# Second attention block of a fused transformer kernel: one 96-row product per head over moved keys and queries, values spread over the steps, and splits moved in the first block

## The reference, cut to what matters

```
x = layer_norm(hidden, ln1_w, ln1_b)                      # 8 x 100 x 512
q = (x   @ q_w + q_b).reshape(B, 100, 16, 32)
k = (ctx @ k_w + k_b).reshape(B, 361, 16, 32)
v = (ctx @ v_w + v_b).reshape(B, 361, 16, 32)
attn = softmax(where(mask, q k^T / sqrt(32), min))
hidden = (attn v) @ cproj_w + cproj_b + hidden
out = hidden + gelu(layer_norm(hidden, ln2_w, ln2_b) @ fc_w + fc_b) @ proj_w + proj_b
```

## Time and profile before

| | |
|---|---|
| median of 3 runs | 2333.56 us (2332.52 to 2339.51) |
| the profiled execution's own time | 2332.67 us |
| its span | 2330.9 us |
| mean granted TensorE clock | 0.985 of full speed |
| PE, DVE, ACT, POOL busy | 95%, 69%, 51%, 41% of the span |
| second block's logits, first to last | 1822.2 to 2159.7 us |

### The profile page before, as it was taken

The page is one execution under the profiler, slowest core; times in us unless marked ns, Lnnn a source line. Parts: engine busy times, 40 slices in busy tenths (PEclk is TensorE's granted clock), DMA queues, the critical chain, the costliest instruction groups (busy, mean ns, idle before and its releaser), DMA issues.

```text
span 2330.9 us, 37139 instructions
## 1 busy us (share of the span) xinstructions
PE 2206.4 (95%) x12724; PEld 2143.7 (92%) x12724; DVE 1603.5 (69%) x3636; ACT 1185.0 (51%) x2834; POOL 944.6 (41%) x903
## 2 busy tenths in 40 slices
PE   7999998999999899999989999999999899888899
PEld 6999998999999899999989999999989788887899
DVE  6767777777777777777776767777574585577443
ACT  4555555555555555555555545565233565466332
POOL 3313444242343424234341424422899132222487
PEclk8999999999999999999999999999999999999999
DMA  3646454554645455465544545554433312111243
GB/s 132 139 81 148 98 110 97 119 120 83 143 107 102 101 116 123 81 148 104 117 103 97 123 95 135 105 118 66 151 108 111 85 46 78 42 42 29 59 124 112
DMA packets 137494, 238.69 MB, mean 102 GB/s; under 512 B 32992, under 2 KB 75104, under 8 KB 137312
## 3 DMA queue, kind: packets, MB, share of 16 engines
q1 hardware_dynamic: 137312, 236.32, 44.8%
HBM read 214.96 MB, written 4.92 MB: 94 GB/s over the span
## 4 chain that ended last, share of the span: by engine, by line
PE 82%; DVE 8%; ACT 4%; DMA 2%; issue 2%; POOL 1%; SPq 1%; POOLq 0%; DVEq 0%; ACTq 0%
PE bank L777 78%; PE bank L865 3%; DVE ctxT L1435 1%; DMA ctxN_raw<-in_ctx 1%; PE bank L1054 1%; DVE hT L1431 1%; DVE ln_c L1485 1%; DVE prob L1601 1%; DVE lnb L1478 1%; POOL mring L699 1%; DVE part L1435 1%; ACT ctxT L1181 0%; DVE pT L1435 0%; ACT qs L1181 0%; ACT ctxN L1181 0%
## 5 line engine op out<-in xcount | busy, mean ns | idle before, releaser
L777 PE MATMUL bank<-ctxT,kring 128*128 128x362 f32 x3456 | 627.7, 329 | 1.1 <-DVE ctxT L1435 1.1
L697 POOL TENSOR_SCALAR mring<-stage 128x512 fp32r<-128x512 f32 x325 | 230.9, 711 | 943.9 <-PE bank L777 810.8
L777 PEld LDWEIGHTS bank<-ctxT,kring 128*128 128x128 f32 x3456 | 585.3, 189 | 3.7 <-issue 1.6
L777 PE MATMUL bank<-pT,ctxN 128*128 128x400 f32 (+1 forms) x2304 | 474.6, 352 | 21.1 <-DVE U L1435 21.1
L699 POOL TENSOR_TENSOR mring<-stage,mring 128x512 fp32r<-128x512 f32 x325 | 443.6, 1365 | 27.1
L777 PEld LDWEIGHTS bank<-pT,ctxN 128*128 128x128 f32 (+1 forms) x2304 | 407.4, 189 | 27.2 <-issue 26.0
L777 PE MATMUL bank<-hT,mring 128*128 128x400 f32 x1608 | 326.0, 353 | 26.1 <-DVE hT L1431 23.6
L777 PEld LDWEIGHTS bank<-hT,mring 128*128 128x128 f32 x1608 | 301.6, 193 | 30.0 <-issue 28.1
L777 PE MATMUL bank<-U,mring 128*128 128x400 f32 x1536 | 303.2, 348 | 8.0 <-issue 6.2
L777 PEld LDWEIGHTS bank<-U,mring 128*128 128x128 f32 x1536 | 275.3, 188 | 10.2 <-issue 7.8
L1181 ACT ACTIVATE kT<-bank,cols 128x361 fp32r<-128x361 f32 (+1 forms) x288 | 160.5, 557 | 234.0 <-PE bank L777 234.0
(11 more groups left out here) (102 smaller groups left out, 2988.9 us busy)
## 6 DMA issues: line engine op xcount, KB each, us to landing
ctxT_raw<-in_ctx SPq DMA_DIRECT2D x72, 724.0 KB, 7.3
ctxN_raw<-in_ctx SPq DMA_DIRECT2D x256, 192.0 KB, 3.0
stage<-in_wk SPq DMA_DIRECT2D x64, 256.0 KB, 4.4
stage<-in_wq SPq DMA_DIRECT2D x64, 256.0 KB, 5.1
stage<-in_wv SPq DMA_DIRECT2D x64, 256.0 KB, 4.0
stage<-in_wo SPq DMA_DIRECT2D x64, 256.0 KB, 2.6
stage<-in_fa SPq DMA_DIRECT2D x64, 256.0 KB, 2.6
stage<-in_fb SPq DMA_DIRECT2D x64, 256.0 KB, 2.6
```

Source lines behind the costliest of these rows:

```text
L697: nc.gpsimd.tensor_scalar(hi, src, 1.0, 1.0, ALU.mult, ALU.mult).then_inc(S.w_hi, 1)
L777: mm = pe.matmul(dst, parts_l[a], parts_r[b], start=first and k == 0, stop=last and k == len(order) - 1)
```

## The change

It has two parts that share no code.

**First block.** The high halves of the context that were both made in step n%16 = 3 are made in steps 1 and 2; the two low halves move on DVE from before the four value sums of that step to after the first and after the second. Of the three layer norms `norm_high` goes from steps 11 and 12 to step 10, `norm_low` from steps 11, 12, 13 to 10, 11, 12.

**Second block.** Keys and queries are moved by DMA so that the three part products of one head lie below each other: q3 holds a head's queries three times 32 rows (high, high, low) and k3 its keys (high, low, high), as `PARTS3` says, and one matmul over 96 rows replaces three over 128. For the keys this is `save_k`: 12 DMAs a step, SBUF to SBUF, 32 rows by 362 columns each, issued by SP at the head of its step. Queries come in three DMAs a batch in place of four. Keys run two steps ahead (`AHEAD`), one bank in place of two; values come one row tile a step at heads 2 and 3 (`v1_tile`); value sums follow two steps behind (`BEHIND`) in place of three, three matmuls at each of heads 0 to 2. The keys' weight is loaded raw in the MLP and split by ACT and DVE, and not by POOL. The layer norm sum 7 goes from DVE to POOL. Four projection tiles are due together (step 14). At the end `up` number 34 is done before the projection too.

```diff
@@ queues and tables
-        add(303, "1k", j)
-        add(T_ATT1 + 10 + j, "1c", 0, j)
-        add(T_ATT1 + 29, "1c", 1, j)
+        add(T_ATT1 + 14, "1c", 0, j)
+        add(T_ATT1 + 30, "1c", 1, j)
-    CONTEXT_HIGH[4 * (i_ - 1) + [3, 1, 1, 1][(i_ - 1) % 4]] = i_
     for k_ in range(2):
+        CONTEXT_HIGH.setdefault(4 * (i_ - 1) + [1 + k_, 1, 1, 1][(i_ - 1) % 4], []).append((i_, k_))
-        APPLIED = [[], [], [0, 1, 2], []]
-        S_CPROJ, CPROJ = NS // 2 + 3, [[], [0], [1, 2, 3], []]
-        S_Q1 = 9
+        VALUES1 = [[], [], [0, 1], [2, 3]]
+        AHEAD, BEHIND = 2, 2
+        S_CPROJ = NS // 2 + BEHIND
+        S_Q1 = 10
+        PARTS3 = [(0, 0, 0), (1, 0, 1), (2, 1, 0)]
@@ SP
+            def save_k(s):
+                sp.wait_ge(S.k1_lo, s + 1)
+                if s >= 2:
+                    sp.wait_ge(S.s1_mm, HG * (s - 2) + HG)
+                else:
+                    sp.wait_ge(S.o_mm, DC * GN)
                 for i in range(HG):
+                    for k, _, k_part in PARTS3:
+                        sp.dma_start(f32(k3[k * HD1:(k + 1) * HD1, s % 2, i, :]),
+                                     f32(kT[i * HD1:(i + 1) * HD1, s % 2, k_part, :])).then_inc(S.k3_in[s % 2], 16)
-            for s in range(NS + 3):
+            save_k(0)
+            for s in range(NS + BEHIND):
+                if 1 <= s + AHEAD - 1 < NS:
+                    save_k(s + AHEAD - 1)
+                if s >= BEHIND + 1:
+                    save_heads(s - BEHIND - 1)
                 load_jobs(jobs_due(T_ATT1 + s - 1) + STAGE)
...
-                if s % 4 == 1 and s // 4 + 1 in range(2, BATCH):
+                if s % 4 == 3 and s // 4 + 1 in range(2, BATCH):
                     load_q(s // 4 + 1)
-                if s >= 4:
-                    save_heads(s - 4)
@@ PE
             def logits1(u):
                 if i == 0:
-                    pe.wait_ge(S.k1_hi, s + 1)
-                    pe.wait_ge(S.k1_lo, s + 1)
+                    pe.wait_ge(S.k3_in[s % 2], 16 * 12 * (s // 2 + 1))
-                split_mms(bank[2 + u % 2][0:LQ, 0:LT],
-                          [q_masked[:, b % 2, i, p_, j * LQ:(j + 1) * LQ] for p_ in range(2)],
-                          [kT[:, s % 2, p_, :] for p_ in range(2)], True, True).then_inc(S.s1_mm, 1)
+                pe.matmul(bank[2 + u % 2][0:LQ, 0:LT], q3[:, b % 2, i, j * LQ:(j + 1) * LQ], k3[:, s % 2, i, :],
+                          start=True, stop=True).then_inc(S.s1_mm, 1)
+            for s in range(NS + BEHIND):
                 for i in range(HG):
+                    u = s * HG + i
...
+                    if s + AHEAD < NS and KEYS1[i]:
+                        keys1(s + AHEAD, KEYS1[i])
+                    if s >= BEHIND and i < TC:
+                        value_sums1(s - BEHIND, i)
+                    if v1_tile(s) and VALUES1[i]:
+                        values1(*v1_tile(s), VALUES1[i])
                     if s == S_CPROJ:
+                        project1(0, i)
@@ ACT
             def key1_high(s):
                 act.wait_ge(S.k1_mm, s + 1)
+                if s >= 2:
+                    act.wait_ge(S.k3_in[s % 2], 16 * 12 * (s // 2))
-                if norm_at(n, 11):
-                    norm_high(norm_at(n, 11), (0, 1))
-                if norm_at(n, 12):
-                    norm_high(norm_at(n, 12), (2, 3))
+                if norm_at(n, 10):
+                    norm_high(norm_at(n, 10))
@@ DVE
-                if norm_at(n, 13):
-                    norm_low(norm_at(n, 13), (2, 3))
                     if kind == "u":
                         value_sum_low(G, k)
+                        for i, j in CONTEXT_LOW.get(n, ()):
+                            if k == 12 + j and n % 16 == 3:
+                                context_low(i, j)
+                if norm_at(n, 10):
+                    norm_low(norm_at(n, 10), (0, 1))
                 if norm_at(n, 11):
-                    norm_low(norm_at(n, 11), (0,))
+                    norm_low(norm_at(n, 11), (2,))
                 if norm_at(n, 12):
-                    norm_low(norm_at(n, 12), (1,))
+                    norm_low(norm_at(n, 12), (3,))
```

More of the change, by code:

```diff
@@ L170 @@
 IN_W1 = {("a", 1): 0, ("b", 0): 1, ("a", 2): 2, **{("1c", 1, j): j for j in range(4)}}
-IN_M = [key for _, key in JOBS if key not in IN_W1 and key[0] not in ("k", "1k")]
+IN_M = [key for _, key in JOBS if key not in IN_W1 and key[0] != "k"]
 M_AT = {key: i for i, key in enumerate(IN_M)}
@@ L374, in build @@
         S.at_in = sem("at_in")
+        S.k3_in = [sem(f"k3_in{k}") for k in range(2)]
+        S.k1w_in = sem("k1w_in")
+        S.k1w_hi = sem("k1w_hi")
+        S.k1w_lo = sem("k1w_lo")
         S.v1w_in = sem("v1w_in")
@@ L598, in load_values_weight, with load_keys_weight @@
                     sp.dma_start(w1_raw[:, j, 1, :], T["1v"][j]).then_inc(S.v1w_in, 16)
+            def load_keys_weight():
+                sp.wait_ge(S.k_mm, NU)
+                for j in range(4):
+                    sp.dma_start(kring_raw[:, j, 1, :], T["1k"][j]).then_inc(S.k1w_in, 16)
             def load_mask(b):
@@ L956, in down @@
                 for c in range(DC):
-                    mm = split_mms(bank[ACC[c]][:, 0:ROWS], w_cols(key, c), [part[:, f % 2, p_, :] for p_ in range(2)],
+                    mm = split_mms(bank[ACC[c]][:, 0:ROWS], w_cols(key, c),
+                                   [part[f // NF][:, f % 2, p_, :] for p_ in range(2)],
                                    f % FF == 0, f % FF == FF - 1)
@@ L975, in queries1, with values1 @@
                     pe.wait_ge(S.q1_lo, Q)
[L976 to L977 removed]
                 for c in range(DC):
[L979 removed]
+                    mm = split_mms(q1_bank(Q), w_cols(key, c), [hT_c(hT0, 0, c), hT_c(hT0, 1, c)], c == 0, c == DC - 1)
                 mm.then_inc(S.q1_mm, 1)
[L982 to L985, removed]
+            def values1(b, t, chunks):
@@ L1009, in values1 @@
+                for c in chunks:
+                    mm = split_mms(v1_bank(b, t)[0:TK[t], :], ctxT_c(i, c, t * P, t * P + TK[t]),
+                                   two(w1[:, c]), c == 0, c == DC - 1)
+                if c == DC - 1:
                     mm.then_inc(S.v1_mm, 1)
@@ L1303, in value_weight_high, with key_weight_high, context_high @@
                 high(w1[:, j, 0, :], w1_raw[:, j, 1, :]).then_inc(S.v1w_hi, 1)
-            def context_high(i):
+            def key_weight_high(j):
+                act.wait_ge(S.k1w_in, 64)
+                high(kring[:, j, 0, :], kring_raw[:, j, 1, :]).then_inc(S.k1w_hi, 1)
+            def context_high(i, halves=(0, 1)):
                 act.wait_ge(S.ctxT_in[i % 2], 16 * (i // 2 + 1))
-                for k in range(2):
+                for k in halves:
                     a = slice(k * HALF_T, (k + 1) * HALF_T)
@@ L1338, in _ @@
                         natural_high(un)
-                if n in CONTEXT_HIGH and n % 4 == 3:
-                    context_high(CONTEXT_HIGH[n])
                 if norm_at(n, VAR_STEP):
@@ L1352, in _ @@
                         natural_high(un)
-                if n in CONTEXT_HIGH and n % 4 != 3:
-                    context_high(CONTEXT_HIGH[n])
+                for i, k in CONTEXT_HIGH.get(n, ()):
+                    context_high(i, (k,))
                 if norm_at(n, 3):
@@ L1371, in mlp_steps @@
                         value_weight_high(F - 13)
+                    if m == 0 and F in range(25, 29):
+                        key_weight_high(F - 25)
                     if m == 0 and F in (10, 11):
@@ L1729, in mlp_steps @@
                         value_weight_low(F - 14)
+                    if m == 0 and F in range(26, 30):
+                        key_weight_low(F - 26)
                     if F % FF == FF - 1:
```

306 lines of the change are left out of this document (158 added, 148 removed).

## The result

| | before | after |
|---|---|---|
| median of 4 runs | 2335.75 us | 2354.95 us (2349.21 to 2359.9) |
| ratio, 95% interval | | 1.0081 (1.0049 to 1.0113) |
| profiled span | 2330.9 us | 2347.4 us |
| first block's last value sum | 1627.5 | 1587.1 |
| first logits of the second block | 1822.2 | 1788.0 |

The change made the kernel 0.8% slower; the forecast was 2271, in a range of 2240 to 2316. By the profiles the first block gained 40.4 us of a forecast 46.0. The second block lost all of it and more.

What follows compares the result with a forecast made beforehand. TensorE's waits were taken to bound the first block and, after the change, SP's DMA issues the second. 2332.67 less 20.3 (context halves), 25.7 (layer norms) and 16.1 (second block) gave 2271 us, range 2240 to 2316.

Steps and rivals of the forecast that it cites:

- First block: First block: moving context halves and layer norm parts removes TensorE's waits on U and hT; 20.3 and 25.7 us.
- context halves: First block: moving the halves removes TensorE's wait on U in 15 groups, 1.35 us each, 20.3 us gained.
- norms: First block: three layer norm waits on hT go, 17.3 us, and the slow stretches behind them, 8.4; 25.7 us gained.
- TensorE's cut: Second block: two of three logit matmuls a head go, 1.5 us a step, but alone not on the path.
- p = 0.53: Second block: price in us of one save_k issue on SP, twelve a step, 6.36 us.
- rival 2: Second block: dear save_k issues at 0.60 to 0.64 us, the heads' price; 2297 to 2312 us, chance 0.19.
- Step 3 to 29: Second block: 27 steps of SP issuing saves of keys (6.36 us) and heads (2.55 us), 240.6 us.
- ACT's wait for heads: Second block: ACT's value_sum1_high is held by saved heads, but within SP's period; no period under about 8.8 us.
- Rival 1: Second block: cheap save_k issues at 0.45 us, 30 us less, 2241 us; chance 0.18.
- Rival 3: Second block: DVE and ACT bound it if SP needs under 7.8 us a step; 2236 us, chance 0.05.
- Rival 4: Second block: slower, save_k at the loaded price of 0.76 us an issue; 2357 us, chance 0.07.
- Tail: Second block's end, last step's logits to projection: 28.0 us for 24.9, less 2.2 for an up; net loss 0.9.

Runs made afterwards that it cites:

- first_only: The kernel before with only the first block's moves (context halves and layer norm parts): 2295.5 us, ratio 0.9832.
- first_ctx: The kernel before with only the first block's context halves moved, layer norms left: 2311.7 us, ratio 0.9903.
- three_qv: The changed kernel with three logit matmuls a head, no saves of keys, keys one step ahead, queries' load and value tiles earlier: 2267.6 us.
- bounce_qv: The changed kernel with a step's keys saved to DRAM by one DMA, fetched by three behind the heads' saves, queries' load and value tiles earlier: 2266.4 us.
- half_k: The changed kernel with queries' load and value tiles earlier, each save of keys copying only half a row: 2342.6 us.
- fetch12: The changed kernel with queries' load and value tiles earlier, keys saved to DRAM by one DMA, fetched by twelve behind the heads' saves: 2323.2 us.
- swap: The changed kernel with SP issuing the saves of heads ahead of those of keys in each step: 2366.2 us, ratio 1.0139.
- swap_qv: The changed kernel with queries' load and value tiles earlier, and heads saved ahead of keys: 2342.4 us, ratio 1.0027.

## Why the prediction was wrong, point by point

- **First block, 46.0 forecast, 40.2 measured.** The context halves were right: 20.3 forecast, 20.7 measured alone. The norms were worth some 19.5 for 25.7: 3.8 us of waits on hT stayed and 4.2 on the low key are new, a small form of "another input late at the same place". `first_only` shows both waits, 9.3 and 4.2 us, and `first_ctx` has no such wait on the key, so it came with the norms' moves.
- **Second block, TensorE's cut: right.** "The cut alone is not on the path": `three_qv` and `bounce_qv` are 1 us apart.
- **The price p = 0.53: wrong, 0.63.** This is the first step that failed. The prediction had the heads' row, four in 2.55 us, SBUF to SBUF and in a row, 0.64 each, and argued it down by a lone p_row issue and two runs a row. `half_k` and `fetch12` show that for these rows the source matters and the bytes don't, and the heads' row was the nearest in source, destination and place in a burst. The p_row issue has its source in SBUF too, but it is another kind of transfer: it spreads one row over 128 partitions, and its landing took 9.1 us at the median where the heads' took 1.9. The prediction's own rule, 3.7 us per 0.01, makes 2308 of 0.63: rival 2, and still inside the range. The Trainium skill's page "Perfetto Trace Analysis", section "What "DMA-bound" means", tells of a track solid with issues, where the time goes into issuing and not into moving. The second half is borne out (half the bytes, 591 ns as before). The track was not solid: SP waited 38.0 us of the 347.2.
- **"Step 3 to 29: 27 x (6.36 + 2.55)", a solid track: wrong.** This is the second step that failed, the larger fault in the method, and the one that took the time out of the range. It gave SP nothing but its issues, two waits for weights and 13 for the projection. SP waited for logits in 12 places, 30.8 us. The 12.7 of the projection was forecast (13); the others weren't. A part of them comes from `load_q`: the prediction charged its 18 issues at 0.45 and never asked when they land. The change had put them behind a step's saves and just ahead of the logits that read them, and those logits release SP's next save. The third value tile, copied at the head of the step that needs it, was missed in the same way. The runs price the two at 6 us each while SP is loaded. The profiled execution, 2349.2, lies 78.6 us over the forecast of 2270.6, and SP's rows place it: some 44 are the price of all the saves, long bursts included, 6 the first block, 18 the waits for logits beyond the projection's, and 11 other waits and the gaps between DMAs. That is where the time lies, not what each piece is worth: of the last two, 29 together, the runs price only the two shifts, 13.5, and no run took the rest apart.
- **ACT's wait for heads within SP's period: right.** It was there, 52.2 us, and taking it away (`swap`, `swap_qv`) gave nothing. Before the projection TensorE waited 5.0 us for the heads where 8 were forecast.
- **Rival 1 (p = 0.45)** has its price in `fetch12`, with a landing added: 2323, not 2241. **Rival 3's** place was reached by `bounce_qv`: 2266 for 2236; its shortest steps, past the first two, are 8.0 to 8.2 us where 7.8 was taken, and its mean step is 9.6 where that sum, with its extras, has 8.8. **Rival 4** had the result, 2357, for the wrong reason: p was 0.64 in the mean (0.72 only in its longest bursts), not 0.76, and waits did the rest.
- **Tail:** 0.9 lost was forecast; from the last step's logits to the end it is 174.9 us for 178.1 before, 3.2 gained.

The range failed because each bound moved p alone. None had SP waiting longer than in the main line.

## What to carry over

Price an instruction by the row that matches it in source, destination and position in a burst, and don't argue it down. Where a change makes a queue the bound, write out its loop: for each DMA in it, the step whose result it waits for, when it lands, and who needs it first; a load moved to the end of a step costs its landing, not its issue. When several waits of an engine are each covered by the same queue, removing them one by one shows little (13.5 us for 76); lighten the queue first, then they count (32 us).

## What the runs showed of the hardware

- An issue on SP takes 591 ns with source and destination in SBUF and 421 from DRAM, both 32 rows of 1448 bytes; with 724 bytes still 591. One DMA of 128 rows from SBUF to DRAM took 338 (median of 32 in `bounce_qv`). The saves of queries, SBUF to DRAM as well but in 512 runs, took 507 (median of 16 in the changed kernel), so the places alone don't set the price:

```profile
L617 SPq DMA_DIRECT2D k_parts<-kT x32: 327/338/1465, 1781.0 to 2079.4; - x32
```

- Fewer matmuls in the same time can leave TensorE at a lower clock: in 357 us of the second block the granted clock was 0.97 in `three_qv` with 334 us of busy time, and 0.91 in `bounce_qv` with 315. It was 0.96 before (1822.2 to 2177.6 us) and 0.86 in the changed kernel (1787.9 to 2196.4), which waits most. All are means between the levels of 1.2 GHz (0.5) and 2.4 (1.0).
